# Projections of a five-layer attention kernel in three one-pass products instead of one four-byte product

## What is computed

```python
def attention(x, ctx, Wq, bq, Wk, bk, Wv, bv, Wo, bo):      # 16 heads of 16 columns
    q, k, v = x @ Wq + bq, ctx @ Wk + bk, ctx @ Wv + bv
    p = softmax(q @ k.T / 4)                                 # per head
    return (p @ v) @ Wo + bo
x = norm(attention(x, ctx, L0, mask) + x) * g + b            # L0
x = norm(attention(x, ctx, L1) + x) * gamma + beta           # L1
n = norm(x) * ln1_g + ln1_b
x = x + attention(n, n, SELF, causal)                        # SELF
x = x + attention(norm(x) * ln2_g + ln2_b, ctx, CROSS)       # CROSS
x = x + relu((norm(x) * ln3_g + ln3_b) @ f_w1 + f_b1) @ f_w2 + f_b2   # FFN
x = x + attention(norm(x) * g + b, ctx, L3 with W rounded to -gamma, 0, gamma)   # L3
```

## Time and profile before

| | us |
|---|---|
| Median of 3 runs | 1464.13 (1464.09 to 1464.85) |
| The profiled execution | 1464.82 |
| Its span, first to last instruction | 1463.1 |
| PE busy | 1404.4 |
| DVE busy | 1005.1 |
| ACT busy | 783.9 |
| POOL busy | 481.4 |

### The profile page before, as it was taken

How to read it: one execution, slowest core, us unless ns; L and a number is a source line. 1 busy time by engine, 2 the same in 40 slices (tenths; PEclk the granted TensorE clock), 3 DMA queues, 4 the chain that set the end, 5 groups by cost and what they waited for, 6 DMA issues and landing times.

```text
span 1463.1 us, 42292 instructions
## 1 busy us (share of the span) xinstructions
PE 1404.4 (96%) x18408; PEld 1138.3 (78%) x18408; DVE 1005.1 (69%) x1895; ACT 783.9 (54%) x1305; POOL 481.4 (33%) x511
## 2 busy tenths in 40 slices
PE   4999999999999999999999999999989999899998
PEld 3777777777777777777777777778989999677775
DVE  3667677698787776666666677778686666656664
ACT  2565655655656555555555666665423334565663
POOL 6122213344444453332332221112485555000100
PEclk8999999999999999999999999999999999999999
DMA  7101000100000000000000100000000000000000
GB/s 290 37 26 43 23 26 15 52 9 16 9 9 9 31 16 2 2 2 2 2 2 16 45 9 9 15 9 23 30 1 1 2 1 8 16 30 30 30 24 30
DMA packets 14000, 34.79 MB, mean 24 GB/s; under 512 B 2167, under 2 KB 7543, under 8 KB 12407
## 3 DMA queue, kind: packets, MB, share of 16 engines
q1 hardware_dynamic: 13815, 32.09, 6.7%
HBM read 27.89 MB, written 4.19 MB: 22 GB/s over the span
## 4 chain that ended last, share of the span: by engine, by line
PE 82%; DVE 8%; ACT 5%; issue 2%; DMA 1%; POOL 1%; SPq 0%; DVEq 0%; ACTq 0%; POOLq 0%
PE ps L549 10%; PE ps L718 9%; PE ps L655 7%; PE ps L682 7%; PE ps L600 6%; PE ps L731 5%; PE ps L699 5%; PE ps L572 5%; PE ps L744 5%; PE ps L560 5%; ACT s_PU L841 4%; DVE s_nm L966 4%; PE ps L660 2%; PE ps L679 2%; PE ps L539 2%
## 5 line engine op out<-in xcount | busy, mean ns | idle before, releaser
L966 DVE TENSOR_REDUCE s_nm<-ps 128x8 fp32r<-128x960 f32 (+1 forms) x352 | 395.2, 1168 | 132.8 <-PE ps L600 74.8
L841 ACT ACTIVATE s_PU<-ps 120x1024 f32<-120x1024 f32 (+1 forms) x288 | 273.1, 1028 | 161.2 <-PE ps L660 161.2
L1105 POOL TENSOR_TENSOR s_xs<-s_xs,s_rowv 128x512 f32<-128x512 f32 x96 | 126.4, 1317 | 508.8 <-DVE s_nt L909 460.9
L655 PE MATMUL ps<-s_Qs,s_KH 32*120 32x256 f32 (+2 forms) x4608 | 180.3, 286 | 5.9 <-DVE s_xs L987 2.8
L655 PEld LDWEIGHTS ps<-s_Qs,s_KH 32*120 32x120 f32 (+1 forms) x4608 | 150.3, 181 | 41.2 <-issue 31.2
L549 PE MATMUL ps<-s_xT,s_W 128*128 128x256 f32 x640 | 163.4, 399 | 10.6 <-DMA s_xT<-x_t 9.4
L850 ACT ACTIVATE s_Os<-ps 128x512 f32<-128x512 f32 x160 | 94.4, 596 | 128.5 <-PE ps L682 83.4
L718 PE MATMUL ps<-s_W,s_oT 128*128 128x256 f32 x640 | 156.6, 387 | 1.3 <-ACT s_oT L857 0.9
L794 ACT ACTIVATE s_Qs<-ps,s_colv 128x256 fp32r<-128x256 f32 x160 | 67.2, 472 | 148.5 <-PE ps L549 148.5
L549 PEld LDWEIGHTS ps<-s_xT,s_W 128*128 128x128 f32 x640 | 118.2, 195 | 35.9 <-issue 11.1
L682 PE MATMUL ps<-s_PU,s_Vp 120*32 120x256 f32 x2048 | 126.3, 383 | 6.8 <-DVE s_nm L966 5.5
(11 more groups left out here) (89 smaller groups left out, 2334.6 us busy)
## 6 DMA issues: line engine op xcount, KB each, us to landing
s_cT<-ctx_t SPq DMA_DIRECT2D x32, 240.0 KB, 2.6
s_W<-w_att SPq DMA_DIRECT2D x5, 1024.0 KB, 5.0
s_xs<-x_nat SPq DMA_DIRECT2D x4, 1024.0 KB, 11.8
s_xT<-x_t SPq DMA_DIRECT2D x16, 256.0 KB, 2.7
out<-s_xs SPq DMA_DIRECT2D x16, 256.0 KB, 2.0
s_rowv<-rows SPq DMA_DIRECT2D x6, 512.0 KB, 4.2
s_W<-w_ff SPq DMA_DIRECT2D x2, 1024.0 KB, 5.1
s_mi<-mask SPq DMA_DIRECT2D x8, 120.0 KB, 3.7
```

Of the source, the lines that this page charges most:

```text
L655: e.matmul(banks[j][0:n, wide * x:wide * x + wide], kz[row[j], lk, g, c, k0:k0 + n], q[row[j], lq, g, qs_], start=(x == 0 and y_ == 0), st ...
L841: t = e.activation(P_of(i, k)[0:n, :, :], pair("B", i, k)[0:n, :, :], ACT.Exp, scale=0.25)
L966: e.tensor_reduce(o, v, AX.X, ALU.max, negate=True).then_inc(sem["max"])
L1105: e.tensor_tensor(xs[:, b, :, :], xs[:, b, :, :], row2(layer, 0), ALU.add).then_inc(sem["pool"])
```

## The change

Every projection (`Q`, `K`, `V`, `O`) is computed like `F1` and `F2` before: both operands are split into a rounded fp32r part and a rest, and `PARTS` names three one-pass products, which accumulate in the same bank. A stage has 12 products in place of 4.

```diff
                 for g in range(2):
-                    for k in range(2):
-                        t = e.matmul(m[:, g * 256:g * 256 + 256], wv(layer, 0)[:, k, 128 * g:128 * g + 128], xT_of(i)[:, k, :],
-                                     start=(k == 0), stop=(k == 1))
+                    for c, (cw, cx) in enumerate(PARTS):
+                        for k in range(2):
+                            t = e.matmul(m[:, g * 256:g * 256 + 256], wv(layer, cw, 0)[:, k, 128 * g:128 * g + 128], xT_of(i)[:, cx, k, :],
+                                         start=(c == 0 and k == 0), stop=(c == 2 and k == 1))
                 t.then_inc(sem["Q"])
```

```diff
+            def OTlo(i):
+                o = oT[slot("oT", i)]
+                w.wait_ge(sem["OTh"], nth("OTh", i))
+                e.tensor_tensor(o[:, 1, :, :].rearrange("p a n -> p (a n)"), bankM("OT", i),
+                                o[:, 0, :, :].bitcast(f32).rearrange("p a n -> p (a n)"), ALU.subtract).then_inc(sem["OTl"])
+            def Clo(i):
+                c = cT[slot("cT", i)]
+                w.wait_ge(sem["Ch"], nth("Ch", i))
+                behind()
+                e.tensor_tensor(c[:, 1, :, :], cf[:, :, :], c[:, 0, :, :].bitcast(f32), ALU.subtract).then_inc(sem["pool"])
```

```diff
+            def wb(n, m):
+                o, src, shift = bankM("wb", n, m), ws_of(n, m), fold_b(n)
+                empty("wb", n, m)
...
+                    for g in range(2):
+                        for k in range(2):
+                            t = e.matmul(o[:, g:g + 1], src[:, k, 128 * g:128 * g + 128], shift[:, k:k + 1], start=(k == 0), stop=(k == 1))
```

SBUF room for this comes from `On`, which has one buffer in place of two, and from `X` and the copies `W1`, `W2`. The planner's tables `WANT` and `LONG` are new (`LONG` gives `Q`, `V` and `O` 1.43 in place of 1.73), and with them the order of every engine:

```diff
-STAY = 0.121
+STAY = 0.158
```

More of the change, by code:

```diff
@@ L11 @@
 PAIRED = ("L0", "L1", "CROSS", "L3")
-WSLOT = {"L0": 0, "L1": 1, "SELF": 2, "CROSS": 0, "F1": 1, "F2": 2, "L3": 0}
+SETS = ["L0", "L1", "SELF", "CROSS", "F1", "F2", "L3"]
+WSLOT = {n: k % 3 for k, n in enumerate(SETS)}
+FOLDED = {"SELF": (0, 1, 2), "CROSS": (0,), "F1": (0, 1, 2, 3), "F2": (), "L3": (0,), "L0": (), "L1": ()}
 PARTS = [(0, 0), (0, 1), (1, 0)]
 MANY = {"MI": 1, "S": 2}
[L17 to L20, removed]
@@ L23 @@
[L23 to L27, removed]
+WANT = dict(Xl=-1.31, xT=-3, cT=-4, mi=-4, bo=-0.54, N=2.96, T=-0.96, Q=0.18, Qh=2.79, Ql=0.43, K=-0.21, Kh=1.11, Kl=0.59,
+            K0=-0.06, V=0.68, Ve=2.57, mf=-0.74, A=0.45, max=0.14, M=-0.05, mTe=0.55, B=0.86, exp=0.68, cap=1.77, PV=1.79,
+            PVe=2.42, ON=2.33, ONe=1.93, OT=2.98, O=-0.19, y=2.45, st=6.41, rs=0.41, ln=1.69, lng=4.37, F1=-0.76, Fa=0.46,
+            Fv=-2.33, Hl=0.58, F2=2.43, out=2.2, Th=-2.92, Tl=-1.16, OTh=-0.54, OTl=1.4, Ch=-3, Cl=-3)
@@ new lines @@
+LONG = dict(xT=.6, cT=.6, mi=.6, ws=.6, row=.6, x=.6, out=.6, bo=1.3, N=.65, T=.44, Th=.48, Tl=.62, Xl=1.3, Q=1.43, Qh=.74, Ql=.8, K=1.35, K0=.87,
+            Kh=1.17, Kl=1.25, V=1.43, Ve=.67, Ch=.5, Cl=1.25, mf=.3, A=.69, max=1.07, M=.22, mTe=.28, B=.95, exp=.91, cap=.67, PV=.87,
+            PVe=.48, ON=.44, ONe=.64, OT=.44, OTh=.48, OTl=.62, O=1.43, y=.6, st=1.05, rs=1.04, ln=.65, lng=2.6, F1=2.86, Fa=.72, Fv=.79,
+            Hl=2.43, F2=2.86, wb=.5, wa=.2, wg=.75, Wh=.52, Wl=1.3, qs=.57, qm=.05, qa=1.5, qw=4.1)
@@ L29 @@
+LAND = dict(xT=2.5, cT=2.5, mi=2.5, ws=3.0, row=3.5, x=7.0, out=3.0)
 ARRAY = dict(A="rows", B="rows", PV="columns")
 TURN = .19
-STAY = 0.121
+STAY = 0.158
 NEXT = .11
@@ L228, in make_plan @@
                 add("POOL", "bo", after=[("T", i, 0), ("row", nr, 0)])
-                add("ACT", "Te", after=[("T", i, 0)], long=.48)
             else:
@@ L867, in Fa @@
                 w.wait_ge(sem["F1"], nth("F1", i, u))
+                w.wait_ge(sem["wa"], max(nth("wa", "F1", m) for m in range(4)))
                 for j in range(2):
@@ L1177, in _, with load_ws @@
                 e.dma_start(tile, src).then_inc(sem["d_cst"], 16)
-            def load_w(layer):
-                after = {"CROSS": "L0", "F1": "L1", "F2": "SELF", "L3": "CROSS"}.get(layer)
-                if after:
-                    w.wait_ge(sem["O"], max(nth("O", B * LAYERS.index(after) + b) for b in range(B)))
-                src = {"F1": w_ff1, "F2": w_ff2}.get(layer)
-                if src is None:
-                    src = w_att[ATT.index(layer)]
-                e.dma_start(W[WSLOT[layer]][:, :], src).then_inc(sem[f"d_w{layer}"], 16)
+            def load_ws(n, m):
+                was = ring["ws"].before[n, m]
+                if was is not None:
+                    w.wait_ge(*w_ready(*was))
+                e.dma_start(ws_of(n, m)[:, :, :], weights[SETS.index(n), m]).then_inc(dma_ops["ws", n, m][0], 16)
             def row(n):
```

396 lines of the change are left out of this document (228 added, 168 removed).

## The result

| | before | after |
|---|---|---|
| Median of 5 runs beside each other, us | 1464.6 | 1471.3 |
| Ratio, with its 95% interval | | 1.0043 (1.0029 to 1.0058) |
| Span of the profiled execution, us | 1463.1 | 1469.5 |
| PE busy | 1404.4 | 1372.2 |
| Span less PE busy | 58.7 | 97.3 |

What follows compares the result with a forecast made beforehand. PE's list was taken to set the time. From 1464.8 us: projections -73, format changes +18, folding +10, chain to O +9, VectorE +5, start +2, waits -5, so -34; forecast 1430, range 1402 to 1453.

Steps and rivals of the forecast that it cites:

- the count of its switches: On PE's list: 118 more changes between whole array, row groups and column groups, at 0.155 us each, lose 18 us.

Runs made afterwards that it cites:

- e4: The changed kernel in its order, but with fp32 projection products and without VectorE's 160 rest subtractions; 1514.1 us, 49.5 more than the kernel before.
- g1: The whole changed kernel, same instructions, in another order from a search over the planner's tables; 1419.6 us, 45 less than the kernel before.

## What to carry to other kernels

Where every engine works off a fixed list and one edit makes the planner write a new one, the new list is a change of its own, and its price isn't in the count of its switches: cost the waits on the second engine as well, from the new order, unit by unit. Before such a change is judged or thrown away, run it with the old work in the new order (as e4) and with the new work in a searched order (as g1): here the first says +49.5, the second -45. And look for operations that disturb one another, since POOL at 38% of its time was enough to make PE wait. Whether a planner that knows of this finds a better order wasn't tried.
